# The slot table's half rows: two multiplications on GpSimd, comparisons at other places in VectorE's order

## The chip, the cores and the metric

The kernel runs on one core of a Trainium2 chip. The metric is the device time of the whole kernel in microseconds (us), the median of several runs. A core has TensorE (PE in the profile; its weight loads are PEld), VectorE (DVE), ScalarE (ACT), GpSimd (POOL) and SyncE (SP), which only issues DMAs here. Each works through its own list of instructions in order and waits for the others on semaphores.

## The reference, cut to what matters

Three layers act on a batch of 64 x 64 tokens of width 256: attention over a context, gated linear attention, and a feed-forward layer with one shared expert and seven routed ones, of which each token takes the two best. The change lies in the third:

```python
shared_out = _expert(x, shared_gate, shared_up, shared_down)
logits = x @ Wr * routing_bias
scores, idx = top_k(sigmoid(logits), TOPK)          # TOPK = 2
scores = scores / scores.sum(-1, keepdims=True)
...
combined = combined + _expert(xf, routed_gate[e], routed_up[e], routed_down[e]) * weights[:, e:e + 1]
```

The kernel does not run every expert over every token. It sorts the 2 x 4096 (token, choice) pairs by expert into slots, runs each expert over its own slots, and adds the weighted results.

## The kernel before, in words

**Stages.** Up to about 980 us the kernel runs attention and gated attention as a software pipeline over 32 pairs of sequences; in it all engines are busy, GpSimd too (its step function, L516 to L611). Then it runs the feed-forward layer in tiles of R = 256 rows. Tiles 0 to 9 (below FIRST = 10) are the shared expert's, tiles 10 to 47 (FIRST to MID) are NSLOT = 38 slot tiles of the routed experts, and six more shared tiles follow. At the end the routed results are loaded back and added (combine, L1958).

**A tile.** HID = 704 hidden columns are six blocks of 128, in two halves of three. For each half TensorE makes the gate products and the up products (up, L994, matmuls at L990), ScalarE the silu (L1341), VectorE the product of both (hidden, L1747: L1753, and in half 1 also L1757). ScalarE copies it to f16 (hidden_high, its copy helper at L1080), and VectorE subtracts that copy to get the f16 rest (hidden_low, L1761: L1766, and in half 1 L1770). TensorE then multiplies both by the down weights (down, L1009: L1017 to L1022) and VectorE adds the result to the residual (shared_result, L1885) or hands it out (result, L1892). In tile t TensorE does up half 0, down of tile t-1, up half 1. Its up products of half 0 wait for hidden half 1 of tile t-1, those of half 1 for hidden half 0 of tile t, and down of tile t-1 for hidden_low half 1 of tile t-1.

**Expert weights.** While the shared tiles run, the routed experts' weights come in as 28 pieces. SP loads a piece (load_chunk, L447 to L466) once the piece that held its place has been split, ScalarE makes its high half (L1363), VectorE its low half, the residue (chunk_low, L1901). `CHUNKS_AT = (0, 2, 2, 3, 3, ...)` says how many pieces tile t handles; chunks(t, 0) is the first two of them, chunks(t, 1) the rest. SP also issues the transposed loads of the tiles' rows (L474) between them.

**The slot table.** Routing runs on VectorE as a chain of small instructions, each joined to the next by link, which counts the semaphore route_step up and waits for it (L1785 to L1846). It ends with the slot of every pair, cut in a lane (r_lane, 0 to 127) and a half tile (r_half, 0 to 75). From these, for each choice c in 0 and 1, VectorE writes two f16 tables: lanes_of (L1856) compares 32 x 128 lanes with a row of numbers, half_of (L1851) does the same with 32 x 76 half tiles. half_rows (L1860) then multiplies the second by the row of the token in each partition, a pointer scalar, and half_tiles (L1864) multiplies it in place by the number of the token's tile. TensorE multiplies lane and half tables, 64 matmuls (L1054), after tile 3 (`TABLE = 4`); before them it waits for lane_hot_ready, for `route_step >= ROUTE_HOT` and for the shared result of tile 2 (y_ready), and behind them for slots_read. read_slots (L1870 to L1879) copies what they give and turns it into the row numbers of every slot. Its last instruction signals table_ready, on which GpSimd waits (L652) before its gathers (L638) and scatters (L647), and SP before it loads certain pieces.

**VectorE's order.** It is written out by hand; for tiles 1 to 3 it is the loop at L1925, which the change reorders:

```python
for t in range(1, TABLE):
    hidden(t, 0)
    chunks(t, 0)
    shared_result(t - 1, t - 1)
    hidden_low(t, 0)
    if t <= TOPK:
        lanes_of(t - 1)
        half_of(t - 1)
    chunks(t, 1)
    hidden(t, 1)
    hidden_low(t, 1)
    if t <= TOPK:
        half_rows(t - 1)
        half_tiles(t - 1)
```

**Also touched.** split_weights (L1415) on VectorE splits the gated attention's weights in its first stage; between high and low half it waits on gla_hi_ready (L1431, L1432).

Of the kernel before, what the change touches and what calls it, by code (L numbers as in the profile page):

```python
# [6 lines left out]
ALU = mybir.AluOpType  # L7
# [23 lines left out]
NE, TOPK = 7, 2  # L31
# [3 lines left out]
NSLOT = (NB * SQ * TOPK + NE * (R - 1)) // R  # L35
# [15 lines left out]
W_SCALE = 2.0 ** 6  # L51
# [56 lines left out]
def bc(ap, axis, n):  # L108

    v = ap.unsqueeze(axis)  # L110
    shape = list(v.shape)
    shape[axis] = n
    return v.to_broadcast(shape)
# [16 lines left out]
def program(nc, stack, x, ctx_in, pad, xWq, xbq, xWk, xbk, xWv, xbv, xWo, xbo, gWq, gWk, gWg1, gWg2, gWv,  # L130
# [28 lines left out]
    def const(name):  # L159
        lo, hi = CONST[name]  # L160
        return cst[:, lo:hi]
# [154 lines left out]
    S = {}  # L316
    for name in """
        a_done a_ready av_done0 av_done1 av_ready0 av_ready1 chunk_hi_ready chunk_lo_ready cleared consts_loaded
        ctx_high_ready ctx_loaded ctx_low_ready ctx_turned cum_ready dec_exp_k dec_exp_q dec_k_ready dec_ready
        down_done exp_done0 exp_done1 fill_ready first_stored g_gated_ready g_norm_ready g_sq_ready g_v_ready  # L320
        gate_bias gate_done gate_inv gate_silu gla_hi_ready gla_lo_ready gn_t_ready gn_turned go_done go_ready
        gproj_done gs_rstd gs_var heads_t_ready0 heads_t_ready1 heads_turned0 heads_turned1 hid_hi_ready hid_lo_ready
        hid_ready k_heads_ready k_prod_ready k_rot_ready k_swap_ready k_t_ready k_turned kg_abs_ready kg_done
        kg_ln_ready kv_done kv_high kv_loaded kv_ready kv_split lane_hot_ready last_store log_gate_ready logits_done
        logits_ready low_t_ready masks_ready max_ready0 max_ready1 probs_hi_ready0 probs_hi_ready1 probs_lo_ready00
        probs_lo_ready01 probs_lo_ready02 probs_lo_ready03 probs_lo_ready1 probs_turned0 probs_turned1 proj_done
        q_done q_heads_ready q_loaded q_nat_ready q_prod_ready q_rot_ready q_swap_ready q_t_ready q_turned qkl_done
        qs_ready ref_ready route_exp route_mm route_step scores_done0 scores_done1 shared_hi shared_lo shared_loaded
        silu_ready slot_mm slots_loaded slots_read sum_step table_ready up_done v_hi_ready v_split vg_done waits_met
        weights_loaded wv_step x1_ready x1_rstd_ready x1_stat_ready x1n_hi_ready x1n_lo_ready x1n_ready x1n_turned  # L330
        x2_ready x2_rstd_ready x2_stat_ready x2n_ready x2n_split x2n_t_ready x2n_turned x_res_ready x_rstd_ready
        x_stat_ready xn_ready xn_t_ready xn_turned y_ready y_stored
    """.split():
        S[name] = sem(name)
# [177 lines left out]
    def _(pool):  # L512
# [130 lines left out]
        def scatter(t):  # L643
            pool.wait_ge(S["y_ready"], t + 1)
            for a in range(2):
                at = 2 * (t - FIRST) + a
                pool.indirect_dma_start(  # L647
                    out=choice_out,
                    out_offset=bass.IndirectOffsetOnAxis(ap=row_out.bitcast(U32)[:, at:at + 1], axis=0),
                    in_=e_y[:, a, :], in_offset=None).then_inc(S["y_stored"], 16)  # L650

        pool.wait_ge(S["table_ready"], 1)  # L652
        for t in range(FIRST, MID):
# [20 lines left out]
    def _(pe):  # L674
# [372 lines left out]


        pe.wait_ge(S["lane_hot_ready"], TOPK)
        pe.wait_ge(S["route_step"], ROUTE_HOT)  # L1050
        pe.wait_ge(S["y_ready"], TABLE - 1)
        for c in range(TOPK):
            for t in range(NTILE):
# [338 lines left out]
    def _(dve):  # L1392
# [22 lines left out]
        def split_weights():  # L1415
            dve.wait_ge(S["weights_loaded"], 16 * WEIGHT_DMAS)
            v.tensor_scalar(bias_s[0:SQ, 3 * D:4 * D], b_g[0:SQ, :], W_SCALE, None, ALU.mult).then_inc(S["gate_bias"], 1)
            dve.wait_ge(S["gate_bias"], 1)
            v.scalar_tensor_tensor(out=bias_s[32:SQ, 3 * D:4 * D], in0=b_g[32:SQ, :], scalar=W_SCALE,
                                   in1=bias_s[32:SQ, 3 * D:4 * D], op0=ALU.mult, op1=ALU.subtract)\  # L1420
                .then_inc(S["gate_bias"], 1)
            w_v = w_gvg[:, :, 0:D].rearrange("p k (h c) -> p k h c", c=GV)
            head_mean = g_stat[:, 0:DK, :]
            v.tensor_reduce(head_mean, w_v, AX.X, ALU.add).then_inc(S["wv_step"], 1)
            dve.wait_ge(S["wv_step"], 1)
            v.tensor_scalar(head_mean, head_mean, 1.0 / GV, None, ALU.mult).then_inc(S["wv_step"], 1)
            dve.wait_ge(S["wv_step"], 2)
            v.tensor_tensor(w_v, w_v, bc(head_mean, 3, GV), ALU.subtract).then_inc(S["wv_step"], 1)
            dve.wait_ge(S["wv_step"], 3)
            for k, (w, (high, low)) in enumerate(((w_gqk, w_gqk_s), (w_g1, w_g1_s), (w_gvg, w_gvg_s))):  # L1430
                v.tensor_scalar(high, w, W_SCALE, None, ALU.mult).then_inc(S["gla_hi_ready"], 1)  # L1431
                dve.wait_ge(S["gla_hi_ready"], k + 1)  # L1432
                v.scalar_tensor_tensor(out=low, in0=w, scalar=W_SCALE, in1=high, op0=ALU.mult, op1=ALU.subtract)\
                    .then_inc(S["gla_lo_ready"], 1)

# [340 lines left out]
        def link(ins):  # L1776

            ins.then_inc(S["route_step"], 1)
            count[0] += 1
            dve.wait_ge(S["route_step"], count[0])  # L1780
# [73 lines left out]
        def lanes_of(c):  # L1854

            v.tensor_tensor(lane_hot[:, c, :, :], bc(r_lane[:, c, :], 2, P), bc(const("iota"), 1, NTILE), ALU.is_equal)\  # L1856
                .then_inc(S["lane_hot_ready"], 1)

        def half_rows(c):
            link(v.tensor_scalar(half_hot[:, c, :, 0, :], half_hot[:, c, :, 1, :], const("rowid")[:, c:c + 1], None,  # L1860
                                 ALU.mult))

        def half_tiles(c):
            link(v.tensor_tensor(half_hot[:, c, :, 1, :], half_hot[:, c, :, 1, :], bc(const("tnum"), 2, 2 * NSLOT),  # L1864
                                 ALU.mult))

        def read_slots():

            dve.wait_ge(S["slot_mm"], 1)
# [35 lines left out]
        def chunks(t, part):  # L1905
            for n in part_of(chunks_of(t), part):
                chunk_low(n)
# [17 lines left out]
# [3 lines that stand above are left out]
            shared_result(t - 1, t - 1)  # L1928
            hidden_low(t, 0)
            if t <= TOPK:  # L1930
                lanes_of(t - 1)
                half_of(t - 1)
            chunks(t, 1)
            hidden(t, 1)
            hidden_low(t, 1)
            if t <= TOPK:
                half_rows(t - 1)
                half_tiles(t - 1)
        assert count[0] == ROUTE_HOT
        read_slots()  # L1940
        for t in range(TABLE, FIRST):
# [56 lines left out]
BOUND = 60.0  # L1998
ROUTE_SELECTED = 3 + 5 * TOPK + 1 + 2
ROUTE_PARTS = ROUTE_SELECTED + 4 + 2 + NE + 6 + 3 + 2 * TOPK + 5  # L2000
ROUTE_HOT = ROUTE_PARTS + 5 + 3 * TOPK

# [29 lines left out]
```

## Time and profile before

| | |
|---|---|
| median of 3 runs | 1656.41 us |
| the runs | 1653.59, 1656.41, 1656.85 us |
| the profiled execution | 1657.05 us |
| its span | 1655.0 us |
| mean granted TensorE clock | 0.972 |
| TensorE busy | 1546.1 us, 93% |
| VectorE busy | 1222.5 us, 74% |
| ScalarE busy | 969.6 us, 59% |
| GpSimd busy | 855.7 us, 52% |

The span runs from the first to the last instruction; the time has 2.05 us more around it. Busy time is the sum of an engine's instructions over the whole span; it doesn't say which engine sets the end in a stretch. In a timeline row the first number is the start from the span's beginning, the second the duration; "x18" is the number of instructions merged in the row, and the bracket gives the time for which the engine sat idle before it and the instruction that ended the wait. The granted clock is the share of TensorE's full speed (2.4 GHz) that it was given.

### The profile page before, as it was taken

What the parts mean: (1) busy time and instruction counts of PE and PEld (TensorE: products, weight loads), DVE (VectorE), ACT (ScalarE), POOL (GpSimd) and SP (SyncE); (2) the same over time, 40 slices, a digit from 0 to 9 for tenths busy, and PEclk for the clock granted to TensorE, in tenths of its full rate; (3) what the DMA queues carried; (4) which work ended last, traced back from release to release, by engine and by line L of the source; (5) the groups of instructions that cost most, each with busy time, mean ns of one, the idle gap of its engine ahead of it and who ended that gap; (6) DMA issues with size and microseconds to landing.
All of it is one profiled execution on the core that took longest, in us unless ns stands there. A gap on an engine that the chain in (4) does not pass through costs nothing.

```text
span 1655.0 us, 46407 instructions
## 1 busy us (share of the span) xinstructions
PE 1546.1 (93%) x17788; PEld 1158.4 (70%) x17788; DVE 1222.5 (74%) x2413; ACT 969.6 (59%) x2585; POOL 855.7 (52%) x913
## 2 busy tenths in 40 slices
PE   2789999999999999999999867899999999999987
PEld 0457676667676767676767645787888888888865
DVE  1789999999999999999999749774444444444457
ACT  2587888788888888888888622462322222222221
POOL 3776777777777778787877220002333333333210
PEclk9899999999999999999999958999999999999999
DMA  7121322122232222131311123452233222222172
GB/s 188 44 68 35 64 43 71 43 54 59 53 61 49 65 46 68 43 71 41 73 38 36 18 86 58 135 162 72 75 66 72 75 68 71 73 70 71 52 261 71
DMA packets 201986, 118.77 MB, mean 72 GB/s; under 512 B 151696, under 2 KB 190048, under 8 KB 201776
## 3 DMA queue, kind: packets, MB, share of 16 engines
q1 hardware_dynamic: 191024, 82.64, 21.9%
q0 software_dynamic: 10752, 33.17, 5.8%
q8 instruction: 151, 2.47, 0.6%
q14 instruction: 59, 0.48, 0.1%
HBM read 62.29 MB, written 18.35 MB: 49 GB/s over the span
## 4 chain that ended last, share of the span: by engine, by line
PE 82%; DVE 9%; ACT 2%; issue 2%; DMA 2%; SPq 1%; POOL 1%; DVEq 0%; POOLq 0%
PE ps L990 22%; PE ps L692 18%; PE ps L1017 10%; PE ps L679 10%; PE ps L684 6%; PE ps L712 4%; PE ps L740 3%; PE ps L702 3%; PE ps L707 2%; PE ps L732 1%; PE ps L1022 1%; DMA work<-token_in 1%; ACT experts L1088 1%; DVE experts L1400 1%; DVE x_all L1958 1%
## 5 line engine op out<-in xcount | busy, mean ns | idle before, releaser
L990 PE MATMUL ps<-work,experts 128*128 128x256 f16 x3564 | 410.1, 276 | 35.7 <-DVE work L1757 13.6
L990 PEld LDWEIGHTS ps<-work,experts 128*128 (+1 forms) x3564 | 345.9, 99 | 91.0 <-DVE work L1757 14.1
L1080 ACT ACTIVATE work<-work 128x768 f16<-128x768 f32 (+1 forms) x140 | 104.2, 744 | 379.6 <-PE ps L1022 235.5
L692 PE MATMUL ps<-experts 128*128 128x512 f16 (+3 forms) x2560 | 323.4, 265 | 1.9 <-DMA experts<-work 1.7
L1088 ACT ACTIVATE experts<-ps,experts 128x256 f32<-128x256 f32 x512 | 237.3, 484 | 19.9 <-DVE experts L1400 19.0
L692 PEld LDWEIGHTS ps<-experts 128*128 128x128 f16 (+1 forms) x2560 | 158.9, 97 | 122.2 <-issue 41.1
L638 POOL DMA_INDIRECT work<-token_in,work x76 | 74.3, 978 | 323.8 <-DMA work<-work 232.0
L679 PE MATMUL ps<-cst,experts 128*128 128x128 f32 x1440 | 208.9, 280 | 20.1 <-POOL experts L561 7.0
L1080 ACT ACTIVATE experts<-ps 128x512 f16<-128x512 f32 (+2 forms) x352 | 189.4, 583 | 25.0 <-PE ps L679 23.8
L1017 PE MATMUL ps<-experts,work 128*128 (+1 forms) x1620 | 198.3, 276 | 3.7 <-DVE work L1770 3.7
L679 PEld LDWEIGHTS ps<-cst,experts 128*128 128x128 f32 x1440 | 165.1, 145 | 44.8 <-issue 10.0
L545 POOL TENSOR_TENSOR experts<-experts,cst 128x128 f32<-128x128 f32 x256 | 152.8, 634 | 79.3 <-ACT experts L1223 79.3
L1017 PEld LDWEIGHTS ps<-experts,work 128*128 128x128 f16 x1620 | 155.5, 99 | 29.3 <-DVE work L1770 4.0
L1400 DVE TENSOR_REDUCE experts<-ps 128x2 f32<-128x512 f32 x256 | 164.1, 683 | 14.6 <-PE ps L712 13.3
L1753 DVE SCALAR_TENSOR_TENSOR work<-ps,work 128x768 f32<-128x768 f32 x108 | 89.0, 824 | 104.3 <-ACT work L1341 52.6
L647 POOL DMA_INDIRECT choice_out<-work x76 | 75.6, 995 | 120.4 <-DVE work L1892 108.6
L1766 DVE TENSOR_TENSOR work<-work 128x768 f16<-128x768 f32 x108 | 91.6, 848 | 62.1 <-ACT work L1080 62.1
L1341 ACT ACTIVATE work<-ps 128x768 f32<-128x768 f32 x108 | 87.3, 808 | 72.1 <-PE ps L990 72.0
L1892 DVE TENSOR_SCALAR work<-ps 128x512 f32<-128x512 f32 x38 | 26.3, 692 | 116.5 <-PE ps L1022 110.4
L590 POOL TENSOR_TENSOR experts<-experts 128x1024 f16<-128x1024 f32 x32 | 64.0, 2001 | 93.0 <-ACT experts L1171 93.0
L1088 ACT ACTIVATION_READ_ACCUMULATOR experts<-ps,experts 128x1 f32 x512 | 109.9, 215 | 0.0
L684 PE MATMUL ps<-experts,work 128*128 128x256 f32 (+1 forms) x384 | 86.7, 344 | 3.8 <-issue 1.6
(201 smaller groups left out, 2735.3 us busy)
## 6 DMA issues: line engine op xcount, KB each, us to landing
experts<-in_ctx SPq DMA_DIRECT2D x32, 512.0 KB, 4.7
experts<-choice_out POOLq DMA_DIRECT2D x8, 1024.0 KB, 13.5
experts<-in_x SPq DMA_DIRECT2D x32, 128.0 KB, 2.3
token_in<-experts SPq DMA_DIRECT2D x32, 128.0 KB, 3.3
work<-in_L_ffn_routed_gate SPq DMA_DIRECT2D x8, 352.0 KB, 3.0
work<-in_L_ffn_routed_up SPq DMA_DIRECT2D x8, 320.0 KB, 4.0
out<-x_all POOLq DMA_DIRECT2D x5, 512.0 KB, 3.4
experts<-in_L_ffn_routed_gate SPq DMA_DIRECT2D x6, 352.0 KB, 3.0
```

What stands on the lines that cost most here:

```text
L545: ins = nc.gpsimd.tensor_tensor(dst[:, :, :, e], src[:, :, :, 1 - e], bc(sin[:, t, :, e], 1, H), ALU.mult)
L679: ins = pe.transpose(bank[:, k * P:(k + 1) * P], a, ident)
L684: ins = pe.matmul(bank, lhs[k], rhs[k], start=(k == 0), stop=(k == len(lhs) - 1))
L692: ins = pe.matmul(bank, lhs[a][k], rhs[b][k], start=(first and k == 0 and a + b == 0), stop=(k == len(lhs[0]) - 1 and a == 1))
L990: ins = pe.matmul(out, experts_h[:, e, lo:lo + P], e_rows_t[k][:, b * DK + kk, :], start=(kk == 0 and a + b == 0), stop=(kk == DK - 1 and ...
L1017: pe.matmul(out, e_hid_s[a][:, c, rows], experts_h[:, e, at:at + D], start=(c == 0 and a + b == 0), stop=False)
L1080: nc.scalar.activation(dst, src, ACT.Copy).then_inc(done, 1)
L1088: ins = nc.scalar.activation(probs[b][:, 2 * r + g, :], ps[:, r, g * SK:(g + 1) * SK], ACT.Exp, bias=neg_max[b][:, hp:hp + 1], accum_out=r ...
L1341: nc.scalar.activation(e_silu, ps_flat[:, 512 + half * HALF:512 + (half + 1) * HALF], ACT.Silu, scale=1 / W_SCALE).then_inc(S["silu_ready" ...
L1400: v.tensor_reduce(nm[:, :, r], ps[:, r, :].rearrange("p (g j) -> p g j", g=2), AX.X, ALU.max, negate=True).then_inc(done, 1)
L1753: ins = v.scalar_tensor_tensor(out=e_hid[:, 0:n], in0=ps_flat[:, 2048 + half * HALF:2048 + half * HALF + n], scalar=1 / W_SCALE, in1=e_sil ...
L1766: ins = v.tensor_tensor(low, e_hid[:, 0:n], high, ALU.subtract)
```

## The change

It takes half_rows and half_tiles out of VectorE's list and gives both multiplications, for each choice, to GpSimd, behind its first stage and ahead of its wait for the table. There GpSimd waits for VectorE's half_of through route_step, and for its own first multiplication ahead of the second. TensorE's slot matmuls wait for a new semaphore, half_hot_ready, at four. In VectorE's loop half_of stays where it was, lanes_of moves behind hidden_low of half 1, and chunks(t, 1) moves behind that (only tile 3 has a piece in it). ROUTE_HOT falls by four. split_weights counts its waits on wv_step in place of gla_hi_ready, which is gone.

```diff
+        for c in range(TOPK):
+            pool.wait_ge(S["route_step"], ROUTE_HOT - TOPK + 1 + c)
+            nc.gpsimd.tensor_scalar(half_hot[:, c, :, 0, :], half_hot[:, c, :, 1, :], const("rowid")[:, c:c + 1], None,
+                                    ALU.mult).then_inc(S["half_hot_ready"], 1)
+            pool.wait_ge(S["half_hot_ready"], 2 * c + 1)
+            nc.gpsimd.tensor_tensor(half_hot[:, c, :, 1, :], half_hot[:, c, :, 1, :], bc(const("tnum"), 2, 2 * NSLOT),
+                                    ALU.mult).then_inc(S["half_hot_ready"], 1)
 
         pool.wait_ge(S["table_ready"], 1)
...
         pe.wait_ge(S["lane_hot_ready"], TOPK)
-        pe.wait_ge(S["route_step"], ROUTE_HOT)
+        pe.wait_ge(S["half_hot_ready"], 2 * TOPK)
...
-                v.tensor_scalar(high, w, W_SCALE, None, ALU.mult).then_inc(S["gla_hi_ready"], 1)
-                dve.wait_ge(S["gla_hi_ready"], k + 1)
+                v.tensor_scalar(high, w, W_SCALE, None, ALU.mult).then_inc(S["wv_step"], 1)
+                dve.wait_ge(S["wv_step"], k + 4)
...
-        def half_rows(c):
-            link(v.tensor_scalar(half_hot[:, c, :, 0, :], half_hot[:, c, :, 1, :], const("rowid")[:, c:c + 1], None,
-                                 ALU.mult))
-
-        def half_tiles(c):
-            link(v.tensor_tensor(half_hot[:, c, :, 1, :], half_hot[:, c, :, 1, :], bc(const("tnum"), 2, 2 * NSLOT),
-                                 ALU.mult))
...
             hidden_low(t, 0)
             if t <= TOPK:
-                lanes_of(t - 1)
                 half_of(t - 1)
-            chunks(t, 1)
             hidden(t, 1)
             hidden_low(t, 1)
             if t <= TOPK:
-                half_rows(t - 1)
-                half_tiles(t - 1)
+                lanes_of(t - 1)
+            chunks(t, 1)
...
-ROUTE_HOT = ROUTE_PARTS + 5 + 3 * TOPK
+ROUTE_HOT = ROUTE_PARTS + 5 + TOPK
```

## Rows read from the trace of the kernel before

**Rows 1.** The page, part 1: engine, busy us (share of the span), instructions.
```profile
PE 1546.1 (93%) x17788; PEld 1158.4 (70%) x17788; DVE 1222.5 (74%) x2413; ACT 969.6 (59%) x2585; POOL 855.7 (52%) x913
```

**Rows 2.** Windows: length, busy of PE, PEld, DVE, ACT, POOL, then PEclk, DMA.
```profile
1010.00:1056.00 46.00, 32.00 (x270) 25.78 (x269) 41.83 (x38) 11.96 (x14) 0.00 (x0) 0.85 0.41 98
1056.00:1120.00 64.00, 64.00 (x566) 53.93 (x563) 48.44 (x60) 35.80 (x40) 2.08 (x2) 1.00 0.52 150
```

**Rows 3.** TensorE timeline, tiles 1 to 3: start us, us, engine, line [idle before].
```profile
1009.84 2.12 PE L990 MATMUL ps<-work,experts 128*128 128x256 f16 x18 [0.18 <-ACT work L1341]
1020.81 4.02 PE L990 MATMUL ps<-work,experts 128*128 128x256 f16 x18 [8.85 <-DVE work L1757]
...
1039.52 3.80 PE L990 MATMUL ps<-work,experts 128*128 128x256 f16 x18 [4.74 <-DVE work L1757]
...
1050.56 4.38 PE L1054 MATMUL ps<-experts 128*128 128x152 f16 x64
```

**Rows 4.** VectorE timeline, tiles 1 to 3 and the read of the slots.
```profile
1012.57 4.42 DVE L1856 TENSOR_TENSOR experts<-experts,cst 128x4096 f16<-128x4096 f32 x1
1016.90 2.68 DVE L1851 TENSOR_TENSOR experts<-experts,cst 128x2432 f16<-128x2432 f32 x1
1019.62 0.69 DVE L1753 SCALAR_TENSOR_TENSOR work<-ps,work 128x512 f32<-128x512 f32 x1
...
1022.82 0.85 DVE L1860 TENSOR_SCALAR experts<-experts,cst 128x2432 f16<-128x2432 f16 x1
1023.70 2.69 DVE L1864 TENSOR_TENSOR experts<-experts,cst 128x2432 f16<-128x2432 f16 x1
...
1027.31 1.82 DVE L1901 SCALAR_TENSOR_TENSOR experts<-experts 128x768 f16<-128x768 f32 x2
...
1046.02 1.61 DVE L1901 SCALAR_TENSOR_TENSOR experts<-experts 128x1408 f16<-128x1408 f32 x1
...
1049.08 0.68 DVE L1885 SCALAR_TENSOR_TENSOR x_all<-ps,x_all 128x512 f32<-128x512 f32 x1
...
1054.97 0.32 DVE L1870 COPY experts<-ps 128x152 f32<-128x152 f32 x1 [0.40 <-PE ps L1054]
```

**Rows 5.** TensorE timeline, end of tile 9.
```profile
1127.16 5.77 PE L990 MATMUL ps<-work,experts 128*128 128x256 f16 x36 [3.57 <-issue]
```

**Rows 6.** GpSimd by source line: ns min/median/max, first and last start, form.
```profile
L590 POOL TENSOR_TENSOR experts<-experts x32: 1995/1998/2106, 12.8 to 858.8; 128x1024 f16<-128x1024 f32 x32
...
L600 POOL TENSOR_TENSOR experts<-work,experts x32: 669/795/797, 191.8 to 976.3; 128x256 f16<-128x256 f32 x32
...
L585 POOL TENSOR_SCALAR experts<-experts x32: 615/620/622, 21.2 to 883.5; 128x512 bf16<-128x512 f32 x32
...
L598 POOL TENSOR_SCALAR experts<-work x32: 857/858/1130, 190.9 to 975.3; 128x256 f16<-128x256 f32 x32
...
L605 POOL TENSOR_SCALAR work<-x_all,work x32: 1224/1228/1517, 163.6 to 973.9; 128x256 f32<-128x256 f32 x32
```

**Rows 7.** Source lines and timelines of both engines where their instructions overlap.
```profile
L1500 DVE TENSOR_TENSOR experts<-experts x32: 415/416/2200, 49.9 to 908.9; 128x256 f32<-128x256 f32 x32
...
49.90 2.20 DVE L1500 TENSOR_TENSOR experts<-experts 128x256 f32<-128x256 f32 x1 [0.86 <-POOL experts L569]
...
49.83 1.99 POOL L575 TENSOR_TENSOR work<-experts 128x1024 f16<-128x1024 f32 x1
...
L550 POOL TENSOR_TENSOR work<-work x32: 669/672/4662, 92.5 to 944.1; 128x256 f16<-128x256 f32 x32
...
314.33 4.66 POOL L550 TENSOR_TENSOR work<-work 128x256 f16<-128x256 f32 x1 [0.70 <-ACT work L1080]
...
313.79 4.68 DVE L1743 SCALAR_TENSOR_TENSOR experts<-experts 128x4352 f16<-128x4352 f32 x1
```

**Rows 8.** Timelines of both engines in one step of the first stage.
```profile
613.50 0.68 DVE L1586 TENSOR_TENSOR work<-work 128x512 f32<-128x512 f32 x1
...
612.79 1.23 POOL L605 TENSOR_SCALAR work<-x_all,work 128x256 f32<-128x256 f32 x1
```

More of the change, by code:

```diff
@@ L320, in program @@
         down_done exp_done0 exp_done1 fill_ready first_stored g_gated_ready g_norm_ready g_sq_ready g_v_ready
-        gate_bias gate_done gate_inv gate_silu gla_hi_ready gla_lo_ready gn_t_ready gn_turned go_done go_ready
+        gate_bias gate_done gate_inv gate_silu gla_lo_ready gn_t_ready gn_turned go_done go_ready
         gproj_done gs_rstd gs_var heads_t_ready0 heads_t_ready1 heads_turned0 heads_turned1 hid_hi_ready hid_lo_ready
         hid_ready k_heads_ready k_prod_ready k_rot_ready k_swap_ready k_t_ready k_turned kg_abs_ready kg_done
-        kg_ln_ready kv_done kv_high kv_loaded kv_ready kv_split lane_hot_ready last_store log_gate_ready logits_done
+        kg_ln_ready kv_done kv_high kv_loaded kv_ready kv_split half_hot_ready lane_hot_ready last_store log_gate_ready logits_done
         logits_ready low_t_ready masks_ready max_ready0 max_ready1 probs_hi_ready0 probs_hi_ready1 probs_lo_ready00
```

## The prediction

> **What bounds the kernel now.** The page's first part gives TensorE 93% of the span [rows 1]: its matmuls and its holes set the end. The windows say where the holes are: from 1056 to 1120 it is busy 64.00 of 64 us; in the stretch of the slot table, 1010 to 1056, it works 32.00 of 46, VectorE 41.83 and GpSimd 0.00 [rows 2]. TensorE's timeline shows two large holes there, 8.85 and 4.74 us, both ended by L1757, the second instruction of hidden half 1; after each, 18 matmuls take 4.02 and 3.80 us where 2.12 is usual [rows 3], since the granted clock has dropped (0.85 over the stretch [rows 2]). So VectorE's order in tiles 1 to 3 sets this stretch. Its timeline tells why: lanes_of (4.42) and half_of (2.68) stand ahead of hidden half 1, the two multiplications (0.85 and 2.69) ahead of the next tile's hidden half 0 [rows 4]. In tile 3 the slot matmuls start at 1050.56 [rows 3], behind the shared result (1049.08 + 0.68), and TensorE goes on once L1870 has read them, at 1055.3 [rows 4]. Whatever moves that moment moves the end: the later hole of 3.57 us [rows 5] hangs on a chain of expert pieces that starts from a matmul of its own tile, so it moves along, and so do the piece loads on SP, which wait for VectorE's residues, and the gathers on POOL, which wait for the table.
>
> **The change part by part.** The sum is made in the profiled execution (span 1655.0, time 1657.05, 0.64 above the median of 1656.41); its difference is applied to the median. Times without a unit below are us after 1000.
>
> Semaphore renamed in split_weights: the same instructions and waits, nothing.
>
> Removed from VectorE: 0.85 + 2.69, with issue 3.6 us a choice, 7.2 in all [rows 4]. Moved: lanes_of behind hidden_low half 1, so hidden half 1 comes 4.4 earlier; piece 6 behind hidden half 1 of tile 3, still ahead of the read of the slots.
>
> Added on GpSimd, idle until the table [rows 2], so nothing is queued behind it but the gathers: per choice a one-operation multiplication by a pointer scalar (2432 elements, f16) and a tensor multiplication (2432, f16 by f32). The second is nearest to L590 (1024 elements, one input and the output f16): 1.998 us, against L600's 0.669 at best for 256 a slope of 1.73 ns an element, so 4.45; in proportion it would be 4.75, the upper end; the lower VectorE's own 2.69. The first has no equal. Lower bound: L585's 620 ns for 512 as slope (0.77 ns, above a start of 0.23 us that L600 and L590 leave) with L598's remainder, 2.5 us. Upper: L605, two pointers, 1.228 for 256, in proportion 11.7. L598 has its form (one operation, f16 out), 0.858 for 256: 2.5 us if its excess is a start cost, 6.2 if it is paid per element [rows 6]. I take 4.3, their middle.
>
> Does VectorE keep its pace beside it? Mostly not. L1500 (median 0.416, both inputs in SBUF) once starts 0.07 behind GpSimd's L575 and takes 2.20, until L575 is over; the other way round L550 (median 0.672) takes 4.66 while VectorE's L1743, 4.68 long, runs [rows 7]. So such an instruction and one of GpSimd that reads SBUF exclude each other whole. The Trainium skill says this (SBUF — State Buffer, "Who interferes with whom": an exclusive lock, by order of issue, also against VectorE instructions with two SBUF inputs), and by it the change loses. Against it stands one pair: L1586 keeps its 0.68 though L605 still has half a microsecond to run [rows 8], so the pointer form seems to end its reads well before its end. Hidden and the shared result read PSUM and one SBUF tensor and I don't hold them up; hidden_low, lanes_of, half_of and the pieces' residues I do.
>
> Choice 0. half_of 12.6 to 15.3; hidden half 1 to 16.4, so TensorE resumes 4.4 earlier and ends up(2,0) at 20.4 with the same slow clock. GpSimd's first product 15.4 to 19.7, its reads over at about 19.2. hidden_low(1,1), wanted at 17.4 (ScalarE's copy lies between), gets 19.2 to 20.3; the second product 20.3 to 24.75; lanes_of, wanted at 20.3, is held until 24.6 and ends at 29.0. hidden(2,0) runs 29.0 to 29.9; now it starts at 26.4 (1023.70 + 2.69 [rows 4]). TensorE: down(1) 20.4 to 25, gates to 27, then it waits for hidden(2,0), and reaches up(3,0) at 33.3. VectorE: residues 1.8 [rows 4], shared result 0.7, hidden_low 0.9, half_of 2.7, so 36.0; hidden(2,1) to 37.1, still 2.4 ahead of the 39.5 where its hole ends now [rows 3].
> Choice 1. First product 36.1 to 40.4; hidden_low (wanted 38.1) 39.9 to 41.0; second 41.0 to 45.4; lanes_of 45.3 to 49.65; hidden(3,0) to 50.55; two residues of 1.61 [rows 4], 53.7; shared result, 54.4: the slot matmuls start 3.8 later than now. From the end of that result to L1870 VectorE has 4.8 of work (1049.76 to 1054.97, less a wait of 0.4 [rows 4]), the same in the new order: read done at 59.6 against 55.3. Sum: 4.3 later, **1656.4 + 4.3 = 1660.7 us**.
> If nothing excluded anything, GpSimd's time would be hidden by lanes_of and the residues: its last product would be ready at 29.8 + 8.9 = 38.7, 3 us before it is needed.
>
> **Rivals.**
> No exclusion that counts (these reads are two-byte or broadcast, or GpSimd lets go between parts). Then lanes_of(0) ends at 22.8, hidden(2,0) at 23.7, hidden(2,1) at 30.9, lanes_of(1) at 37.3, the shared result at 41.9, the read at 47.1: 8.1 earlier, 1648.3. Should VectorE only be held for a third of such time, some 5 earlier, 1651.3. For it: rows 8, and holes of 13.6 us as room. Against: rows 7.
> Short first product, 2.5 to 3.5 us, with exclusion. It comes twice on the path, so each microsecond off it is worth two: at 2.5 the sum is 4.3 - 3.6 = +0.7, at 3.5 it is +2.7; about 1658. The Trainium skill (GPSIMD Engine Reference, 4.1) calls one-input work roughly line rate; by it the product would take about 2.5 us, an estimate, and the kernel end near 1657.
> Long first product, paid per element: at 6.2 the sum is 4.3 + 2 x 1.9 = +8.1, 1664.5; with 11.7 it would be 1675, which I hold for unlikely.
> The forecast is slower, so the mechanism on the other side is the first rival; it decides where VectorE is held for less than about 4 us a choice, half of its 8.1 (the forecast has 1.8 for hidden_low and 4.3 for lanes_of). The change not doing what it says would need GpSimd busy at 1015, where it only waits for the table. A loss swallowed at the hole of 1123 I give nothing: its chain moves along.
>
> **How the numbers follow.** About 0.2% (3.3 us) is what a measurement can tell from no change. Forecast case (exclusion, first product 3.5 to 5.5 us, +2.7 to +6.7): 0.35. Short: 0.25. Long: 0.20. No or weak exclusion: 0.20, all of it faster. Slower takes the long case and most of the forecast case, 0.50; same the short one and the rest, 0.30. The range goes from 1649.5, a little past the weak exclusion, to 1666, the long case with the tensor product at its upper end. The forecast case alone has 1659 to 1663.5.
>
> **What would show it.** In the changed profile: L1856 and L1766 far above 4.42 and 0.69 where GpSimd's two new lines run, ending as they end; the first hole ahead of L1757's release shrunk from 8.85 to about 4.5; a new wait of some 3 us for hidden half 0 of tile 2; slot matmuls near 1054, behind the shared result and not behind GpSimd. If the comparison stays at 4.4 beside GpSimd, the exclusion is wrong here and the time is near 1649. If GpSimd's first line is under 3 or over 6 us, the size is wrong and the rivals' sums hold. If the matmuls wait for GpSimd itself, the order is not as I have it.

## The result, and the profile after

The changed kernel takes 1664.84 us (median of 5 runs, 1662.74 to 1667.66), the kernel before 1656.35 (5 runs). The ratio is 1.0053, 95% interval 1.004 to 1.0066: slower, by about 8.5 us (by the interval, 6.6 to 10.9). The profiled execution took 1667.66 us, with a span of 1665.9.

A measure that a single trace gives sharply is needed below: **the stretch**, from the start of hidden half 0 of tile 1 to the end of the read of the slots, both on VectorE. Before it is 1007.16 to 1055.29, 48.13 us (its end: [rows 4]); after it is 1010.73 to 1066.25, 55.52 us, 7.39 more. It has two parts. The first, VectorE's part, in which its own list sets the pace, ends with the shared result of tile 2 (L1885): 42.60 before, 50.02 after. The second is the slot matmuls and their read: 5.53 and 5.50, with matmuls of 4.38 and 4.37; these hang on the clock that TensorE is granted, and below they are not always so short. Behind the read the two traces are alike: 599.7 us to the end of the span in each (1655.0 - 1055.29 and 1665.9 - 1066.25). So the loss is made in the stretch and, between these two traces, arrives in full; over the kernels below the time behind the read lies between 596.1 and 599.9, so a single pair of traces tells this to a few us, and the medians (+8.5) agree with it. The other 3.6 us between the two spans lie ahead of the stretch, where the change does nothing but count on another semaphore; over the kernels below its start lies anywhere from 1005.5 to 1012.2, which is the spread of a run.

The page's first part, and the windows of the stretch and behind it (length, then busy time of PE, PEld, DVE, ACT, POOL, then PEclk, DMA):

```profile
PE 1550.8 (93%) x17788; PEld 1161.2 (70%) x17788; DVE 1231.5 (74%) x2409; ACT 968.7 (58%) x2585; POOL 876.1 (53%) x917
```

```profile
1010.00:1066.00 56.00, 36.65 (x285) 27.18 (x283) 52.62 (x37) 13.27 (x16) 21.55 (x4) 0.88 0.31 75
1066.00:1130.00 64.00, 63.69 (x562) 53.86 (x563) 48.34 (x63) 35.79 (x40) 2.08 (x2) 1.00 0.54 155
```

VectorE was relieved of four instructions (7.1 us, [rows 4]) and is busy for 9.0 us longer over the span than before (1222.5, now 1231.5). That is the riddle and its answer: time in which an instruction has been started but is held counts as busy. The timelines of VectorE and GpSimd in the stretch show which ones (L1774 is hidden_low, before L1766; L1864 is lanes_of, before L1856; L1761 is hidden, before L1753):

```profile
1020.89 4.34 DVE L1774 TENSOR_TENSOR work<-work 128x512 f16<-128x512 f32 x1 [0.91 <-ACT work L1088]
...
1025.69 8.37 DVE L1864 TENSOR_TENSOR experts<-experts,cst 128x4096 f16<-128x4096 f32 x1
1034.10 0.96 DVE L1761 SCALAR_TENSOR_TENSOR work<-ps,work 128x768 f32<-128x768 f32 x1
...
1042.93 4.33 DVE L1774 TENSOR_TENSOR work<-work 128x512 f16<-128x512 f32 x1 [0.91 <-ACT work L1088]
...
1047.72 8.37 DVE L1864 TENSOR_TENSOR experts<-experts,cst 128x4096 f16<-128x4096 f32 x1
...
1060.07 0.68 DVE L1885 SCALAR_TENSOR_TENSOR x_all<-ps,x_all 128x512 f32<-128x512 f32 x1
...
1065.93 0.32 DVE L1870 COPY experts<-ps 128x152 f32<-128x152 f32 x1
...
1018.92 6.43 POOL L654 TENSOR_SCALAR experts<-experts,cst 128x2432 f16<-128x2432 f16 x1 [38.46 <-DVE experts L1859]
1025.43 4.35 POOL L657 TENSOR_TENSOR experts<-experts,cst 128x2432 f16<-128x2432 f16 x1
```

lanes_of takes 8.37 where it took 4.42 [rows 4]: it starts 0.26 behind GpSimd's tensor product, is held until that ends (1029.78), and then has 4.28 of its own. hidden_low takes 4.34 instead of 0.69, held by GpSimd's first product until 0.8 us before that one's end. Both choices show it to within a hundredth. TensorE's holes in the same stretch (timeline; idle in brackets):

```profile
1020.04 3.56 PE L998 MATMUL ps<-work,experts 128*128 128x256 f16 x18 [4.51 <-DVE work L1765]
1025.72 2.76 PE L1025 MATMUL ps<-experts,work 128*128 128x256 f16 x15 [2.12 <-DVE work L1778]
...
1035.11 1.48 PE L998 MATMUL ps<-work,experts 128*128 128x256 f16 x12 [1.55 <-DVE work L1761]
...
1042.08 2.14 PE L998 MATMUL ps<-work,experts 128*128 128x256 f16 x18 [3.18 <-DVE work L1765]
1047.75 3.38 PE L1025 MATMUL ps<-experts,work 128*128 128x256 f16 x15 [3.53 <-DVE work L1778]
...
1060.90 4.37 PE L1062 MATMUL ps<-experts 128*128 128x152 f16 x64 [2.27 <-DVE x_all L1885]
```

The first hole shrank from 8.85 to 4.51 and the second from 4.74 to 3.18 [rows 3], as the new order intends. In their place stand down's waits for the held hidden_low (2.12 and 3.53, ended by L1778), one for hidden half 0, and 2.27 ahead of the slot matmuls, which wait for VectorE's shared result and not for GpSimd, done since 1051.8. All in all TensorE waits longer than before, and this is how the loss reaches the engine that sets the time.

### The profile page after: what moved, and what is told of

Read it like the earlier page. It is cut to its first block, busy times and chain, and to the rows that moved or that the text cites. A ratio compares the mean times of both kernels' runs of the same rounds, so it can differ in the third digit from the quotient of the medians.

```text
span 1665.9 us, 46405 instructions
## 1 busy us (share of the span) xinstructions
PE 1550.8 (93%) x17788; PEld 1161.2 (70%) x17788; DVE 1231.5 (74%) x2409; ACT 968.7 (58%) x2585; POOL 876.1 (53%) x917
## 4 chain that ended last, share of the span: by engine, by line
PE 79%; DVE 11%; issue 3%; ACT 3%; DMA 2%; SPq 1%; POOL 1%; DVEq 0%; POOLq 0%
PE ps L998 21%; PE ps L700 18%; PE ps L687 10%; PE ps L1025 10%; PE ps L692 6%; PE ps L720 4%; PE ps L748 3%; PE ps L710 3%; PE ps L715 2%; PE ps L740 1%; DMA work<-token_in 1%; PE ps L1030 1%; DVE work L1774 1%; ACT experts L1096 1%; DVE experts L1408 1%
## 5 line engine op out<-in xcount | busy, mean ns | idle before, releaser
L1025 PEld LDWEIGHTS ps<-experts,work 128*128 128x128 f16 x1620 | 156.9, 100 | 36.8 <-DVE work L1778 10.2
L1761 DVE SCALAR_TENSOR_TENSOR work<-ps,work 128x768 f32<-128x768 f32 x108 | 89.0, 824 | 104.6 <-PE ps L998 103.7
L1774 DVE TENSOR_TENSOR work<-work 128x768 f16<-128x768 f32 x108 | 98.9, 915 | 61.9 <-ACT work L1088 61.9
```

Source lines behind the costliest of these rows:

```text
L1025: pe.matmul(out, e_hid_s[a][:, c, rows], experts_h[:, e, at:at + D], start=(c == 0 and a + b == 0), stop=False)
L1761: ins = v.scalar_tensor_tensor(out=e_hid[:, 0:n], in0=ps_flat[:, 2048 + half * HALF:2048 + half * HALF + n], scalar=1 / W_SCALE, in1=e_sil ...
L1774: ins = v.tensor_tensor(low, e_hid[:, 0:n], high, ALU.subtract)
```

## The experiments

Theory A: GpSimd's products hold VectorE's instructions that read two SBUF tensors, for their whole length, and the first product is long. Rival B: the new order itself loses (lanes_of now stands ahead of hidden half 0). Rival C: VectorE is slowed by anything that GpSimd does beside it. All diffs are against the changed kernel unless said otherwise.

**The order alone.** GpSimd's block is taken out, both products go back to VectorE behind lanes_of, and TensorE waits for route_step as before.

```diff
             if t <= TOPK:
                 lanes_of(t - 1)
+                half_rows(t - 1)
+                half_tiles(t - 1)
```

> VectorE's new order alone: lanes_of behind hidden_low half 1, but both multiplications stay on VectorE, behind lanes_of; GpSimd does nothing here. 'The stretch' is from the start of hidden half 0 of tile 1 to the end of the read of the slots, in the profile: 48.1 us before, 55.5 after. Theory A (the loss comes from GpSimd's products holding VectorE's instructions with two SBUF inputs): the stretch is bounded by VectorE's own work, which is the same, so 47 to 48.5 us, time within 2 us of the kernel before. Rival B (the order itself costs, since lanes_of now delays the pieces' residues and hidden half 0): most of the loss is here, 53 us or more. L1774-like and L1864-like instructions at 0.69 and 4.4 under A.

Measured: ratio 1.0002 (0.9987 to 1.0017), stretch 48.57. lanes_of is back at 4.43. Rival B falls: VectorE's part is 41.85, even 0.75 shorter than before. The stretch is 0.4 longer all the same, since in this trace the slot matmuls took 6.23 us instead of 4.38, at a granted clock of 0.69:

```profile
1054.21 6.23 PE L1054 MATMUL ps<-experts 128*128 128x152 f16 x64 [1.76 <-DVE x_all L1885]
```

The order doesn't gain much, since VectorE has the same work to do before the slots are read. This kernel is also the one to add up the change from: there VectorE's part is 8.2 longer (50.02 against 41.85), and the rows give it, 15.2 of holding (3.65 and 3.94 for hidden_low and lanes_of, twice each) less the 7.1 of products taken away.

**The products on GpSimd alone,** VectorE in its old order.

```diff
             if t <= TOPK:
+                lanes_of(t - 1)
                 half_of(t - 1)
+            chunks(t, 1)
             hidden(t, 1)
             hidden_low(t, 1)
-            if t <= TOPK:
-                lanes_of(t - 1)
-            chunks(t, 1)
```

> The products on GpSimd, but VectorE's old order (lanes_of and half_of ahead of hidden half 1). Theory A: GpSimd's two products, 6.4 and 4.4 us, now fall beside hidden_low half 1 and the residues of the pieces; each holds one of them: stretch about 54 us, time 5 to 7 us above the kernel before; lanes_of stays 4.4 and a residue of 0.9 takes 4 or more. Rival B (order): as before, 41 to 48 us, faster than or equal to before. Without any exclusion it would be 47.6.

Measured: ratio 1.0038 (1.0023 to 1.0054), stretch 53.81. The timelines of VectorE and GpSimd:

```profile
1020.01 4.34 DVE L1774 TENSOR_TENSOR work<-work 128x512 f16<-128x512 f32 x1 [0.91 <-ACT work L1088]
...
1025.79 4.80 DVE L1901 SCALAR_TENSOR_TENSOR experts<-experts 128x768 f16<-128x768 f32 x2
...
1018.04 6.43 POOL L654 TENSOR_SCALAR experts<-experts,cst 128x2432 f16<-128x2432 f16 x1 [43.04 <-DVE experts L1859]
1024.55 4.35 POOL L657 TENSOR_TENSOR experts<-experts,cst 128x2432 f16<-128x2432 f16 x1
```

Now lanes_of is clear and the residues are held instead (4.80 for two that take 1.82). hidden_low is held as in the change. The loss is where the products are, whoever stands beside them.

**One SBUF input instead of two.** ScalarE first copies the row of numbers into PSUM bank 0, and both comparisons read it there; VectorE waits once for that copy, and nothing else changes.

```diff
+        nc.scalar.activation(ps[:, 0, 0:P], const("iota"), ACT.Copy).then_inc(S["route_exp"], 1)
...
-            v.tensor_tensor(lane_hot[:, c, :, :], bc(r_lane[:, c, :], 2, P), bc(const("iota"), 1, NTILE), ALU.is_equal)\
+            v.tensor_tensor(lane_hot[:, c, :, :], bc(r_lane[:, c, :], 2, P), bc(ps[:, 0, 0:P], 1, NTILE), ALU.is_equal)\
```

> The changed kernel, but the row of numbers that lanes_of and half_of compare with is first copied by ScalarE into PSUM bank 0, so that both comparisons have only one SBUF input; GpSimd's products as in the change. Theory A: lanes_of falls from 8.37 to 4.4 us although GpSimd's tensor product runs beside it at 4.35; hidden_low (two SBUF inputs) is still held, 4.3 us. Stretch about 47.2 us, so about 8 us faster than the change and equal to before within 1 to 2 us. Rival C (VectorE is slowed by anything GpSimd does, or lanes_of waits for it by a semaphore): lanes_of stays at 8.4 and the stretch at 55.5.

Measured: ratio 1.0007 (0.9995 to 1.002), stretch 47.38, 8.1 us shorter than the change. The timelines:

```profile
1021.85 4.34 DVE L1775 TENSOR_TENSOR work<-work 128x512 f16<-128x512 f32 x1 [0.91 <-ACT work L1088]
...
1026.65 4.42 DVE L1867 TENSOR_TENSOR experts<-experts,ps 128x4096 f16<-128x4096 f32 x1
...
1026.39 4.35 POOL L657 TENSOR_TENSOR experts<-experts,cst 128x2432 f16<-128x2432 f16 x1
```

lanes_of and the tensor product now run side by side, each at its own pace, while hidden_low, still with two SBUF inputs, is held as before. Rival C falls, for reads of PSUM.

**GpSimd writes and doesn't read.** The order alone, plus four fills of a scratch row for each choice, for which only the slot matmuls wait.

```diff
+        for c in range(TOPK):
+            pool.wait_ge(S["route_step"], ROUTE_PARTS + 6 + 3 * c)
+            for k in range(4):
+                nc.gpsimd.memset(scratch[:, 0:32 * 76], 0.0).then_inc(S["half_hot_ready"], 1)
+                pool.wait_ge(S["half_hot_ready"], 4 * c + k + 1)
```

> As the run with the new order alone (both products on VectorE), and in addition GpSimd fills a scratch row of 2432 f32 four times for each choice, from the moment half_of is done: it writes and reads nothing. Theory A, in the form that reads exclude: hidden_low stays at 0.69 and lanes_of at 4.4 beside it; the stretch equals that of the new order alone within 0.3 us. Rival D (any GpSimd instruction holds VectorE's two-input ones): hidden_low and lanes_of are stretched to the end of a fill, stretch longer by 2 us or more.

Measured: ratio 1.0009 (0.9998 to 1.002), stretch 49.33. The timelines:

```profile
1016.66 0.69 DVE L1775 TENSOR_TENSOR work<-work 128x512 f16<-128x512 f32 x1 [0.91 <-ACT work L1089]
...
1017.82 4.42 DVE L1865 TENSOR_TENSOR experts<-experts,cst 128x4096 f16<-128x4096 f32 x1
1022.16 1.81 DVE L1869 TENSOR_SCALAR experts<-experts,cst 128x2432 f16<-128x2432 f16 x1
...
1014.65 8.67 POOL L658 MEMSET experts<- 128x2432 f32 x4 [38.38 <-DVE experts L1860]
```

hidden_low and lanes_of keep their pace beside the fills: a GpSimd instruction that doesn't read does not hold the two-input instructions. The expected stretch (within 0.3 of the order alone) was missed by something else: VectorE's own first product, which has one SBUF input and is three times as fast as half_of over as many elements, takes 1.81 and 1.87 instead of 0.85 beside the last fill. That is the 2.0 us by which VectorE's part is longer than with the order alone (43.82 against 41.85); the two stretches differ by only 0.76 because here the slot matmuls took 4.37.

**The first product's instruction on scratch data.** The order alone, plus that instruction once a choice, on data that nobody reads.

```diff
+            if c == 0:
+                nc.gpsimd.memset(scratch_h[:, 0:32 * 152], 1.0).then_inc(S["half_hot_ready"], 1)
...
+            nc.gpsimd.tensor_scalar(two[:, :, 0, :], two[:, :, 1, :], const("rowid")[:, c:c + 1], None,
+                                    ALU.mult).then_inc(S["half_hot_ready"], 1)
```

> As the run with the new order alone (both products on VectorE), and in addition GpSimd makes the first product's instruction (one operation, pointer scalar, 2432 f16, same access pattern) on scratch data, once for each choice from the moment half_of is done. Nothing waits for its data except the slot matmuls, long after. Theory A: 6.43 us long, it holds hidden_low half 1 for 3.7 us a choice: stretch about 54.4 us, 7 us longer than with the order alone; the scratch fill ahead of it in choice 0 may shift its start by the fill's length. Rival D' (only shared data or the semaphores cause the delay): stretch as with the order alone.

Measured: ratio 1.0064 (1.0047 to 1.0082), stretch 58.25, 9.7 over the order alone. The timelines:

```profile
1023.09 7.04 DVE L1873 TENSOR_SCALAR experts<-experts,cst 128x2432 f16<-128x2432 f16 x1
...
1041.72 4.41 DVE L1779 TENSOR_TENSOR work<-work 128x512 f16<-128x512 f32 x1 [0.91 <-ACT work L1093]
...
1019.84 9.64 POOL L661 TENSOR_SCALAR experts<-experts,cst 128x2432 f16<-128x2432 f16 x1
1039.82 6.42 POOL L661 TENSOR_SCALAR experts<-experts,cst 128x2432 f16<-128x2432 f16 x1 [10.34 <-DVE experts L1864]
```

Choice 1 is as expected. In choice 0 the fill pushed the instruction behind the start of lanes_of: this time GpSimd was held (9.64 for 6.43) and afterwards held VectorE's product, 0.85 long, for 6.2 us. The 3.7 and the 6.2 are the 9.9 by which VectorE's part is longer than with the order alone. A read of data that VectorE doesn't touch is enough to make the loss, and more.

**What the first product's length hangs on.** The same, with four forms on scratch data; a single execution (1671.87 us).

> The order alone, and GpSimd makes four tensor_scalar forms on scratch data: pointer, one operation, 1216 elements f16; immediate, one operation, 2432; immediate, two operations (multiply, add), 2432; pointer, one operation, 2432 contiguous. It measures what the first product's length hangs on. If it is paid per element (2.6 ns, as 6.43 for 2432 suggests): 1216 elements take 3.2 to 3.3 us. If a start cost: more. If the one-operation form is the dear one, as 0.858 us for 256 against 0.620 for 512 with two immediate operations suggested: the immediate one-operation form takes about 6.4 us too and the two-operation form about 2.1. If the pointer is dear: the immediate one takes about 2 to 3 us. Contiguous rows: as the strided 6.43.

GpSimd's timeline (fill, then 1216 elements with pointer; 2432 with one immediate operation; with two; contiguous with pointer), and the VectorE row that the second one waits for:

```profile
1016.05 3.51 POOL L658 MEMSET experts<- 128x4096 f32 x1 [38.65 <-DVE experts L1871]
1019.66 7.21 POOL L661 TENSOR_SCALAR experts<-experts,cst 128x1216 f16<-128x1216 f16 x1
1026.96 6.77 POOL L664 TENSOR_SCALAR experts<-experts 128x2432 f16<-128x2432 f16 x1
1042.57 2.22 POOL L667 TENSOR_SCALAR experts<-experts 128x2432 f16<-128x2432 f16 x1 [8.84 <-DVE experts L1871]
1044.89 6.72 POOL L669 TENSOR_SCALAR experts<-experts,cst 128x2432 f16<-128x2432 f16 x1
...
1019.22 4.42 DVE L1876 TENSOR_TENSOR experts<-experts,cst 128x4096 f16<-128x4096 f32 x1
```

The half-length one waited for lanes_of until about 1023.6 and then took 3.2, half of 6.43: the cost is paid per element, 2.6 ns. Pointer or immediate makes no difference (6.77 immediate, 6.72 with the pointer, contiguous; both begin while a VectorE instruction is still running, which may be their few tenths above 6.43). One operation or two does: with two immediates it is 2.22.

**Two operations in the change.** A second operation that adds zero; what is computed stays the same.

```diff
-            nc.gpsimd.tensor_scalar(half_hot[:, c, :, 0, :], half_hot[:, c, :, 1, :], const("rowid")[:, c:c + 1], None,
-                                    ALU.mult).then_inc(S["half_hot_ready"], 1)
+            nc.gpsimd.tensor_scalar(half_hot[:, c, :, 0, :], half_hot[:, c, :, 1, :], const("rowid")[:, c:c + 1], 0.0,
+                                    ALU.mult, ALU.add).then_inc(S["half_hot_ready"], 1)
```

> The changed kernel, but GpSimd's first product is written with two operations (multiply by the pointer scalar, add 0.0), the same result. The forms measured so far: one operation 6.4 to 6.8 us for 2432 with pointer or immediate, two immediate operations 2.22. If the one-operation form alone is dear, the product takes about 2.3 us, hidden_low half 1 is held by the tensor product instead of it or not at all, and the stretch is about 48.7 us, 6.8 shorter than the change, the time near before. If a pointer is dear as well once there are two operations, the product stays above 6 us and the stretch at 55.5 or more.

Measured: ratio 1.0008 (0.9995 to 1.0021), stretch 48.75. The timelines:

```profile
1020.24 4.38 DVE L1778 TENSOR_TENSOR work<-work 64x256 f16<-64x256 f32 x1
1024.65 4.43 DVE L1864 TENSOR_TENSOR experts<-experts,cst 128x4096 f16<-128x4096 f32 x1
...
1017.40 2.29 POOL L654 TENSOR_SCALAR experts<-experts,cst 128x2432 f16<-128x2432 f16 x1 [38.42 <-DVE experts L1859]
1019.77 4.57 POOL L657 TENSOR_TENSOR experts<-experts,cst 128x2432 f16<-128x2432 f16 x1
```

One more operation makes the instruction 2.8 times faster and takes back 6.8 of the 7.4 us of stretch. Now the tensor product slips in between the two halves of hidden_low (L1778, 0.42 alone, takes 4.38), so that lanes_of is free.

**The first product twice,** writing the same values; a single execution (1676.63 us).

> The changed kernel with GpSimd's first product made twice (the same result), to double the suspected cost. Theory A: hidden_low half 1 is held for another 6.5 us in both choices: stretch about 68.6 us, 13 longer than the change, time about 1678. Rival: if the loss were the order's or a fixed cost of having GpSimd involved, the extra 6.5 us are hidden beside lanes_of and hidden half 0 and the stretch stays within 3 us of 55.5.

Stretch 65.74: 10.2 longer than the change and not the expected 13, and 1.0 of this comes with the slot matmuls (6.04 for 4.37). The timelines of VectorE and GpSimd:

```profile
1024.91 9.88 DVE L1867 TENSOR_TENSOR experts<-experts,cst 128x4096 f16<-128x4096 f32 x1
...
1035.69 4.90 DVE L1904 SCALAR_TENSOR_TENSOR experts<-experts 128x768 f16<-128x768 f32 x2
...
1031.25 7.65 POOL L660 TENSOR_TENSOR experts<-experts,cst 128x2432 f16<-128x2432 f16 x1
```

The dose acts on both choices, but where the sum had the second copy hold hidden_low again, hidden_low got in between (4.34 as before) and lanes_of was held instead (9.88, the tensor product waiting behind it), then the residues: 1.5 and 3.1 us more a choice, which make the 9.2 by which VectorE's part grew. The rest of the doubled length passes beside hidden half 0, which nothing holds.

**The first product on ScalarE,** the second on GpSimd behind it.

```diff
+        def half_rows(c):
+            act.wait_ge(S["route_step"], ROUTE_HOT - TOPK + 1 + c)
+            wait(act, S["half_hot_ready"], 2 * c)
+            nc.scalar.activation(half_hot[:, c, :, 0, :], half_hot[:, c, :, 1, :], ACT.Copy,
+                                 scale=const("rowid")[:, c:c + 1]).then_inc(S["half_hot_ready"], 1)
+
         def tile(t, k, first=False):
+            if 2 <= t < 2 + TOPK:
+                half_rows(t - 2)
             silu(t, 0)
```

> The changed kernel with the first product on ScalarE (a copy with the pointer as scale, 2432 f16, estimated 2.3 us) ahead of its silu of tiles 2 and 3; GpSimd makes the second product behind it. Theory A: hidden_low half 1 is free again (0.69), lanes_of is still held by the tensor product of 4.35 us; stretch about 46.5 us, 9 us shorter than the change and 1 to 2 shorter than before; time about 1655. Under rival B (order) it stays above 53.

Measured: ratio 0.9989 (0.9975 to 1.0004), stretch 48.63. The timelines:

```profile
1023.27 4.42 DVE L1869 TENSOR_TENSOR experts<-experts,cst 128x4096 f16<-128x4096 f32 x1
...
1028.60 4.90 DVE L1906 SCALAR_TENSOR_TENSOR experts<-experts 128x768 f16<-128x768 f32 x2
...
1024.37 7.44 POOL L654 TENSOR_TENSOR experts<-experts,cst 128x2432 f16<-128x2432 f16 x1 [43.15 <-ACT experts L1378]
```

hidden_low is free, as expected. lanes_of isn't held, against the expectation: GpSimd starts 1.1 us behind it, is held itself (7.44 for 4.35) and then holds the residues, for 3.1 us a choice. VectorE's part is 41.01, 9.0 shorter than the change, which is what was expected of the whole stretch. The stretch is 2.1 above the expected 46.5 for another reason, the slot matmuls at a granted clock of 0.60:

```profile
1053.10 7.12 PE L1059 MATMUL ps<-experts 128*128 128x152 f16 x64 [3.32 <-DVE x_all L1890]
```

In the change the same matmuls took 4.37 after a wait of 2.27, with the order alone 6.23 after a wait of 1.76. Whether the low clock belongs to a kernel or to the one execution that was traced, no run here shows; the ratio, from ten runs, is the safer number.

**Both remedies.** The last edit together with the one that puts the numbers in PSUM.

> Both remedies in one: first product on ScalarE, second on GpSimd, and the comparisons' numbers in PSUM. Theory A: nothing of VectorE's is held except a piece's residue for about a microsecond, so the 7.2 us of products taken from VectorE come through in full: lanes_of 4.4, stretch about 40.5 us, 7.6 shorter than before; time about 1648.5, faster than both kernels. If the gain is lost again further on (at the hole before the slot tiles), the stretch shrinks and the time does not.

Measured: 1648.62 us, ratio 0.9957 (0.994 to 0.9974), stretch 40.15. This beats both kernels. The timelines of VectorE, GpSimd, ScalarE and TensorE:

```profile
1022.24 4.42 DVE L1872 TENSOR_TENSOR experts<-experts,ps 128x4096 f16<-128x4096 f32 x1
...
1027.45 1.84 DVE L1909 SCALAR_TENSOR_TENSOR experts<-experts 128x768 f16<-128x768 f32 x2
...
1023.35 4.27 POOL L654 TENSOR_TENSOR experts<-experts,cst 128x2432 f16<-128x2432 f16 x1 [42.56 <-ACT experts L1379]
...
1020.96 2.31 ACT L1379 ACTIVATE experts<-experts,cst 128x2432 f16<-128x2432 f16 x1
...
1045.71 4.37 PE L1059 MATMUL ps<-experts 128*128 128x152 f16 x64
```

Nothing of VectorE's is held, not even a residue, of which a microsecond was expected: the stretch is 8.0 shorter than before, and the span behind it again 599.9, so the gain arrives in full.

**The same with VectorE's old order.**

> The version with ScalarE's first product and the comparisons' numbers in PSUM, but with VectorE's old order (lanes_of and half_of ahead of hidden half 1). Theory A with the order as a separate part: the first hole is 8.9 us again and the tensor product falls beside the pieces' residues (two SBUF inputs), holding one of them for 2 to 3 us a choice: stretch about 49 us, 9 longer than with the new order. If the order were worth nothing, it would be near 40 again.

Measured: ratio 1.0017 (1.0006 to 1.0027), stretch 48.46. The residues, two SBUF inputs each, are held in it (VectorE's timeline):

```profile
1029.90 4.12 DVE L1909 SCALAR_TENSOR_TENSOR experts<-experts 128x768 f16<-128x768 f32 x2
```

The stretch is near the 49 expected, though the first hole is 7.24 and not 8.9. So the new order brings no time alone (ratio 1.0002) and 8.3 us of stretch once the products lie elsewhere and hold nobody.

| kernel | stretch, us | of it to the shared result | slot matmuls | ratio to before |
|---|---|---|---|---|
| before | 48.13 | 42.60 | 4.38 | |
| the change | 55.52 | 50.02 | 4.37 | 1.0053 |
| order alone | 48.57 | 41.85 | 6.23 | 1.0002 |
| products on GpSimd alone | 53.81 | 48.65 | 4.37 | 1.0038 |
| order alone, GpSimd fills | 49.33 | 43.82 | 4.37 | 1.0009 |
| order alone, first product on scratch data | 58.25 | 51.74 | 6.01 | 1.0064 |
| change, numbers in PSUM | 47.38 | 41.88 | 4.37 | 1.0007 |
| change, two operations | 48.75 | 43.12 | 4.38 | 1.0008 |
| change, first product twice | 65.74 | 59.20 | 6.04 | |
| change, first product on ScalarE | 48.63 | 41.01 | 7.12 | 0.9989 |
| both remedies | 40.15 | 34.65 | 4.37 | 0.9957 |
| both remedies, old order | 48.46 | 43.30 | 4.37 | 1.0017 |

Each of the three middle columns is from one traced execution.

## Why the prediction was right, and where it was not

- **Direction and mechanism.** It forecast slower, by the exclusion. Shown: lanes_of held whole by the tensor product (8.37), free once one input is in PSUM (4.42), free beside writes (4.42). The rule of the Trainium skill that it leaned on (SBUF — State Buffer, "Who interferes with whom") holds here in the parts that a run tried: reads against two-input instructions, no hold of these by a GpSimd instruction that only writes, and the order of issue. One thing differs: the hold doesn't last for the whole recorded instruction, since hidden_low got going 0.8 us before the first product's end.
- **Size.** 1660.7 was forecast, +4.3; measured +8.5 in the medians and +7.4 in the stretch. The step that was mis-sized is "I take 4.3, their middle" for the first product. It took 6.43. The sum's own rate, two microseconds for each one, makes 4.3 + 2 x 2.1 = 8.6; the rival "long first product" had 6.2 and 1664.5, and the kernel took 1664.84. That both come so near the median is in part luck: step by step only 7.4 of it is there (see the order of the steps), and the rest of the 8.5 lies within the interval. The time is outside the forecast case's own 1659 to 1663.5 (its +6.7 ends at 1663.1); it is in the range only because that reached over the long case, which had a chance of 0.20. The row nearest in form, L598, had said it (2.5 ns an element and 6.2 us, [rows 6]); I averaged that reading with a start cost, of which the half-length form shows nothing (3.2 against half of 6.43).
- **The low end.** The Trainium skill's "roughly line rate" for one-input work (GPSIMD Engine Reference, 4.1) holds for the f16 form with two operations (2.22 and 2.29 us for 2432 elements, near the 2.5 estimated) and not for the one with a single operation, which this kernel uses. L585 in rows 6 has two operations and L598 one, so the difference was in the rows. But L605 there has two operations as well, with two pointers and f32 out, and 4.8 ns an element is the dearest of them: the rows alone didn't tell what decides.
- **The second product** was forecast at 4.45 and took 4.35.
- **The early release.** Rows 8 were read as "the pointer form seems to end its reads well before its end", with half a microsecond; measured, hidden_low gets going 0.8 us before the first product's end.
- **The order of the steps.** Less the 3.57 us by which this execution reaches the stretch later: first product at 15.35 (forecast 15.4), lanes_of of choice 0 ends at 30.5 (29.0), slot matmuls at 57.3 (54.4), read done at 62.7 (59.6), late by some 1.5 us a choice. That is the first product's 2.1 less 0.6: the sum had the tensor product begin only behind hidden_low, 0.6 after the first product's end, and it began 0.08 behind it. So two misses of opposite sign make the 7.4 of the stretch (4.3 + 2 x 1.5 = 7.3). The slot matmuls wait for the shared result, as said. One signal differed: the wait of TensorE for hidden half 0 of tile 2 is 1.55, not some 3, since the longer hold of hidden_low had already delayed down by 2.12.
- **The other side.** The rival "no exclusion" forecast 1648.3 from a sum of 8.1. With the exclusion taken away the kernel took 1648.62, and the stretch shrank by 8.0. That sum was right, for another kernel.
- **Nothing is swallowed further on,** as forecast: 599.7 us behind the read before and after, and a median that is later by 8.5.

Not tried: whether a version without ScalarE's part, with two operations and with GpSimd's start put behind hidden_low, comes as far as the one with both remedies.

## What to carry to other kernels

That GpSimd is idle doesn't make work on it free: while an instruction of it reads SBUF, VectorE's instructions with two SBUF inputs stood still wherever these runs put the two side by side (lanes_of 8.37 for 4.42), and their waiting shows as busy time. Before moving work there, list what VectorE runs beside it by number of SBUF inputs; an input in PSUM (lanes_of back at 4.42), or ScalarE as the new home (2.31 us, nothing held), avoids the hold. And price the instruction by a row of the same form, the number of operations included.

## What the runs showed of the hardware that I had not expected

- A GpSimd tensor_scalar with one operation takes 2.6 ns an element (6.43 us for 2432, 3.2 for 1216), with pointer or immediate; with two operations 0.9 (2.22 immediate, 2.29 with the pointer). This is for f16 in and out; L605, two operations with two pointers and f32 out, has 4.8 [rows 6].
- VectorE's one-input multiplication of f16, 0.85 us alone, is held as well: 1.81 beside a fill that only writes, 7.04 beside a GpSimd multiplication.
- Between two VectorE instructions issued back to back a waiting GpSimd instruction gets in: the 0.42 us second part of hidden_low took 4.38.
- An input in PSUM costs lanes_of nothing: 4.42 either way.
- TensorE's 64 slot matmuls take 4.37 us at a granted clock of 1.00, 6.23 at 0.69 and 7.12 at 0.60: one stretch of one trace can differ by 2.7 us for this alone, which a comparison of single traces must take out first.
